# One kernel, one reordering: dense tile's first products ahead of two statistics, one root for both, the second half's routing four pairs later

## The reference, cut to what matters

```python
x = _layernorm(x + state_space(x))     # x_norm -> silu, sigmoid gates, a scan over time, W_out; it returns x + y
x = _layernorm(x + experts(x))         # 64 experts of 88 inner values, 8 chosen of each token, and a shared one
x = _layernorm(x + attention(x))       # 16 heads
x = _layernorm(x + signed_mlp(x))
# experts:
scores = sigmoid(x @ gate_w.T)                        # tokens x 64
# the four best of eight groups of experts, then the eight best experts in them
topk_w = scores[chosen]; topk_w = topk_w / (sum(topk_w) + 1e-20) * 2.5
routed = sum over the chosen e of topk_w[e] * (silu(x @ Wg[e].T) * (x @ Wu[e].T)) @ Wd[e].T
out = routed + shared_mlp(x)
```

## Time and profile before

| | us |
|---|---|
| median of 3 runs | 871.46 |
| the 3 runs | 866.16, 871.46, 871.61 |
| profiled execution, its own time | 871.87 |
| span of the profiled execution | 870.1 |
| busy in the span: PE / DVE / ACT / POOL | 621.8 / 483.9 / 400.0 / 365.4 |
| mean granted clock of TensorE | 0.844 of full speed |
| dense tile's pairs, first to last instruction of PE | from about 50 to 226 |
| the 56 and the 64 scatters of POOL | from 50 to 125 and from 156 to 237 |

### The profile page before, as it was taken

How to read it: one execution, slowest core, us unless ns; L and a number is a source line. 1 busy time by engine, 2 the same in 40 slices (tenths; PEclk the granted TensorE clock), 3 DMA queues, 4 the chain that set the end, 5 groups by cost and what they waited for, 6 DMA issues and landing times.

```text
span 870.1 us, 13130 instructions
## 1 busy us (share of the span) xinstructions
PE 621.8 (71%) x3712; PEld 388.1 (45%) x3713; DVE 483.9 (56%) x1238; ACT 400.0 (46%) x900; POOL 365.4 (42%) x401
## 2 busy tenths in 40 slices
PE   5671119510179999921978887967978999998995
PEld 2451006310058999921978772222322333343443
DVE  5770105300046666500646579775866888867986
ACT  4420103200034666600535557745755777787651
POOL 4157750677720000175040525787477070013552
PEclk9886558755579999965989977898989999999998
DMA  9999510211103666621555544242142131000001
GB/s 286 367 253 332 173 40 2 87 54 51 48 1 86 174 177 172 183 76 56 160 136 150 150 136 124 71 130 59 47 128 52 29 105 57 1 2 0 2 12 38
DMA packets 98716, 91.52 MB, mean 105 GB/s; under 512 B 9872, under 2 KB 83696, under 8 KB 97776
## 3 DMA queue, kind: packets, MB, share of 16 engines
q1 hardware_dynamic: 90704, 75.01, 29.4%
q0 software_dynamic: 7680, 15.74, 6.3%
q10 hardware_dynamic: 288, 0.23, 0.1%
HBM read 45.14 MB, written 45.61 MB: 104 GB/s over the span
## 4 chain that ended last, share of the span: by engine, by line
PE 51%; another core or an unknown queue 16%; DVE 13%; issue 11%; ACT 4%; POOL 2%; DMA 1%; SPq 0%; POOLq 0%; DVEq 0%; ACTq 0%
PE ps L1617 8%; PE ps L1604 6%; PE ps L1722 6%; PE ps L1732 6%; PE ps L1712 5%; DVE mx L1226 4%; PE ps L1612 3%; PE ps L1627 3%; PE ps L1526 2%; PE ps L1531 2%; ACT big L803 2%; DVE arena L1344 1%; DVE st L900 1%; DVE arena L1336 1%
## 5 line engine op out<-in xcount | busy, mean ns | idle before, releaser
L1226 DVE TENSOR_REDUCE mx<-ps 128x2 f32<-128x1024 f32 x128 | 151.0, 1217 | 51.0 <-PE ps L1712 31.0
L803 ACT ACTIVATE big<-ps 128x512 f32<-128x512 f32 x256 | 141.5, 598 | 68.7 <-PE ps L1722 45.3
L542 POOL DMA_INDIRECT xd<-xt,idx x120 | 116.1, 967 | 70.0 <-issue 35.8
L558 POOL DMA_INDIRECT big<-od,idx x72 | 69.4, 964 | 181.0 <-DMA od<-big 121.1
L1722 PE MATMUL ps<-arena 128*128 128x512 bf16 (+1 forms) x256 | 90.1, 402 | 24.1 <-ACT big L803 12.5
L1531 PE MATMUL ps<-arena,hmT 96*128 96x128 f32 x128 | 27.2, 346 | 112.1 <-issue 107.8
L1148 DVE TENSOR_TENSOR hm<-sg,ps 128x176 f32<-128x176 f32 x124 | 41.7, 336 | 114.3 <-ACT sg L741 82.4
L1617 PE MATMUL ps<-arena,xbT 128*128 x496 | 101.3, 329 | 5.4 <-issue 5.4
L1604 PE MATMUL ps<-arena,hmT 96*128 x496 | 81.1, 288 | 28.5 <-ACT hmT L737 25.7
L731 ACT ACTIVATE big<-ps 128x256 f32<-128x256 f32 x124 | 47.5, 383 | 83.6 <-PE ps L1604 49.8
L1604 PEld LDWEIGHTS ps<-arena,hmT 96*128 96x128 f32 x496 | 68.9, 200 | 32.6 <-issue 31.2
(11 more groups left out here) (222 smaller groups left out, 1087.7 us busy)
## 6 DMA issues: line engine op xcount, KB each, us to landing
big<-xd SPq DMA_DIRECT2D x62, 256.0 KB
od<-big SPq DMA_DIRECT2D x62, 256.0 KB
arena<-scr SPq DMA_DIRECT2D x96, 96.0 KB
xd<-zeros SPq DMA_DIRECT2D x1, 8192.0 KB
xd<-zeros SPq DMA_DIRECT2D x1, 7680.0 KB, 30.7
arena<-w_gu SPq DMA_DIRECT2D x4, 1408.0 KB, 21.1
arena<-w_d SPq DMA_DIRECT2D x4, 768.0 KB, 18.1
scr<-places SPq DMA_DIRECT2D x8, 384.0 KB
```

Of the source, the lines that this page charges most:

```text
L542: pool.indirect_dma_start(out=xd[f], out_offset=bass.IndirectOffsetOnAxis(ap=idx[:, t, k:k + 1], axis=0), in_=xt[:, t], in_offset=None).th ...
L558: pool.indirect_dma_start(out=slot[:, k], out_offset=None, in_=od[f], in_offset=bass.IndirectOffsetOnAxis(ap=idx[:, t, k:k + 1], axis=0)). ...
L803: act.activation(ering[:, HG * (mt % 2) + h], ps[:, 4 + h % 2, :], ACT.Exp, scale=SCALE).then_inc(exp_ready, 1)
L1226: v.tensor_reduce(mx[:, k, TB * h + 2 * a:TB * h + 2 * a + 2], ps[:, 2 * a:2 * a + 2, :], AX_X, ALU.max).then_inc(s1_free, 1)
```

## The change

The sums `2x + mixer` of quarters 2 and 3 are made first (`mix`, with a semaphore s_mix of their own), and their statistics are moved behind the dense pairs 0 and 1. PE's steps 1 and 2 wait for s_mix and no longer for the statistics. One `rstd_of_second_half` makes the roots of both quarters (8 columns instead of 4), after 6 scatters; before there were two, after 2 and 4 scatters. `normalise` of the two quarters moves from pairs 1 and 3 to pairs 5 and 7. All that belongs to the second half in `DENSE_BESIDE` and `ACT_BESIDE` moves four steps on, `ROUTED_FROM` goes from 8 to 12, and the `beside` steps of `route(1)` with it, so that s_eid of half 0 follows pair 11, and the first row numbers of the second half follow pair 28.

```diff
--- before.py
+++ after.py
@@ -86,9 +86,9 @@
     LOADS = {0: (2,), 1: (3,), 2: (4, 5), 3: (6,), 4: (7,), 6: (8, 9), 7: (10,), 8: (11,), 10: (12, 13), 11: (14,), 12: (15,)}
     MINE = MINGLED
-    DENSE_BESIDE = {4: 2, 6: 3, 8: "logits", 20: "places"}
-    ACT_BESIDE = {4: 2, 6: 3, 9: "scores"}
-    ROUTED_FROM = 8
+    DENSE_BESIDE = {8: 2, 10: 3, 12: "logits", 24: "places"}
+    ACT_BESIDE = {8: 2, 10: 3, 13: "scores"}
+    ROUTED_FROM = 12
     WEIGHT_PIECES = 4
     EP = E // WEIGHT_PIECES
     EARLY = NPAIR - 16
@@ -144,7 +144,7 @@
         st = sb("st", [P, NT, 6])
         mv = sb("mv", [P, NT, 2])
         rstd = sb("rstd", [P, NT])
-        minus_half = sb("minus_half", [P, TB])
+        minus_half = sb("minus_half", [P, 2 * TB])
         idf = sb("idf", [P, P])
         idb = sb("idb", [P, P], BF16)
         marks = sb("marks", [P, 2], BF16)
@@ -289,7 +289,7 @@
         th_ready, th_copied, d_ready, acc_done = sem("th_ready"), sem("th_copied"), sem("d_ready"), sem("acc_done")
         dg_ready, dsg_ready, dhm_ready = sem("dg_ready"), sem("dsg_ready"), sem("dhm_ready")
         dth_ready, dth_copied, dense_ready = sem("dth_ready"), sem("dth_copied"), sem("dense_ready")
-        s_pads, s_under = sem("s_pads"), sem("s_under")
+        s_pads, s_under, s_mix = sem("s_pads"), sem("s_under"), sem("s_mix")
         s_qk, s_qks, s_part, s_split = sem("s_qk"), sem("s_qks"), sem("s_part"), sem("s_split")
         s_pw = [sem(f"s_pw{o}") for o in range(2)]
         s_stk = [sem(f"s_stk{r}") for r in range(2 * GB)]
@@ -484,7 +484,14 @@
                 tiles = tiles_of(k)
                 r = rstd[:, tiles]
                 own(pool.tensor_scalar(r, mv[:, tiles, 1], EPS, None, ALU.add))
-                pool.tensor_tensor(r, r, minus_half[:], ALU.pow).then_inc(s_rstd, 1)
+                pool.tensor_tensor(r, r, minus_half[:, 0:TB], ALU.pow).then_inc(s_rstd, 1)
+
+            def rstd_of_second_half():
+
+                pool.wait_ge(s_st, 2 * B)
+                r = rstd[:, NT // 2:NT]
+                own(pool.tensor_scalar(r, mv[:, NT // 2:NT, 1], EPS, None, ALU.add))
+                pool.tensor_tensor(r, r, minus_half[:], ALU.pow).then_inc(s_rstd, 2)
             own(pool.memset(minus_half[:], -0.5))
             own(pool.memset(zeros[:], 0.0))
@@ -534,8 +541,8 @@
                         pool.wait_ge(s_idx, f + 1)
                     for k in range(TOP_K):
                         n = TOP_K * (t - FIRST[f]) + k
-                        if f == 0 and n in (2, 4):
-                            rstd_of(B + 1 + n // 2)
+                        if f == 0 and n == 6:
+                            rstd_of_second_half()
                         flying = AHEAD_ROWS[f]
                         if n >= flying:
                             pool.wait_ge(s_sc[f][n % flying], 16 * (n // flying))
@@ -943,11 +950,20 @@
                     ins = v.tensor_tensor(made[:, h], ps[:, bank, 0:2 * P].rearrange("p (j l) -> p j l", j=2), zT[:, c, h], ALU.mult)
                 ins.then_inc(s_ys, 1)
+            def mixed(q):
+
+                v.wait_ge(s_yo, q + 1)
+                return v.scalar_tensor_tensor(out=tmp[:, TB * q:TB * q + TB], in0=xt[:, TB * q:TB * q + TB], scalar=2.0,
+                                              in1=ps[:, q].rearrange("p (t m) -> p t m", m=M), op0=ALU.mult, op1=ALU.add)
+
             def add_mixer(q):
-                v.wait_ge(s_yo, q + 1)
-                own(v.scalar_tensor_tensor(out=tmp[:, TB * q:TB * q + TB], in0=xt[:, TB * q:TB * q + TB], scalar=2.0,
-                                           in1=ps[:, q].rearrange("p (t m) -> p t m", m=M), op0=ALU.mult, op1=ALU.add))
+
+                own(mixed(q))
                 stats(tmp, B + q)
+
+            def mix(q):
+
+                mixed(q).then_inc(s_mix, 1)
             first_stats(0)
             first_stats(1)
@@ -1063,7 +1079,7 @@
                 if f == 0:
                     gated(2)
                     gated(3)
-                beside(*range(ROUTED_FROM + 10, 22))
+                beside(*range(ROUTED_FROM + 10, ROUTED_FROM + 14))
                 if f == 0:
                     v.wait_ge(s_pos, 1)
                 else:
@@ -1071,34 +1087,39 @@
                 totals = ps[:, LOGITS[0], n * E:(n + 1) * E] if f == 0 else ps[:, 7, 0:E]
                 own(v.tensor_scalar(rows_of[:], totals, (P - 1) / 2.0, WHOLE_BLOCKS, ALU.add, ALU.add))
-                beside(22)
+                beside(ROUTED_FROM + 14)
                 own(v.tensor_tensor_scan(ends[:, 1:E + 1], back[:], rows_of[:], 0.0, ALU.add, ALU.add))
-                beside(23)
+                beside(ROUTED_FROM + 15)
                 v.wait_ge(s_pos, f + 1)
                 own(v.tensor_tensor(ch[:, own_ts], ps[:, LOGITS[f], 0:n * E].rearrange("p (t e) -> p t e", e=E),
                                     ends[:, 0:E].unsqueeze(1).broadcast_to([P, n, E]), ALU.add))
-                beside(24)
+                beside(ROUTED_FROM + 16)
                 own(v.max(dst[:, FIRST[f]], ch[:, FIRST[f]]))
                 v.tensor_scalar(idx[:, FIRST[f]], dst[:, FIRST[f]], -CHOSEN, None, ALU.add).then_inc(s_first, 1)
                 for t in tiles[1:]:
                     ins = v.max(dst[:, t], ch[:, t])
                 own(ins)
-                beside(25)
+                beside(ROUTED_FROM + 17)
                 rest_of = slice(FIRST[f] + 1, FIRST[f] + n)
                 v.tensor_scalar(idx[:, rest_of], dst[:, rest_of], -CHOSEN, None, ALU.add).then_inc(s_idx, 1)
-                beside(26, 27)
+                beside(ROUTED_FROM + 18, ROUTED_FROM + 19)
                 if f == 0:
-                    add_mixer(2)
-                    add_mixer(3)
+                    mix(2)
+                    mix(3)
                     own(v.scalar_tensor_tensor(out=ra[:, 0], in0=rb[:, 0], scalar=TAKEN, in1=sc[:, 0], op0=ALU.is_equal, op1=ALU.mult))
                     own(v.tensor_reduce(cnt[:, 0:1], ra[:, 0], AX_X, ALU.add))
                     own(v.tensor_scalar(cnt[:, 0:1], cnt[:, 0:1], 1e-20, None, ALU.add))
                     own(v.reciprocal(cnt[:, 0:1], cnt[:, 0:1]))
                     own(v.tensor_scalar(rw0[:], ra[:, 0], cnt[:, 0:1], ROUTED_SCALE, ALU.mult, ALU.mult))
                     for i in range(ROUTED_FROM):
-                        if i in (1, 3):
-                            normalise(xt, tmp, B + 2 + i // 2)
+                        if i == 1:
+                            v.wait_ge(s_mix, 2)
+                            stats(tmp, B + 2)
+                        if i == 2:
+                            stats(tmp, B + 3)
+                        if i in (5, 7):
+                            normalise(xt, tmp, B + 2 + i // 6)
                         dense(i)
                 for c in range(COLS[f]):
@@ -1107,7 +1128,7 @@
                     own(v.tensor_reduce(eidf[:, col], ecmp[:], AX_X, ALU.add))
                     own(v.tensor_scalar(eid[:, col], eidf[:, col], float(E - 1), None, ALU.min))
                 v.sem_inc(s_eid, 1)
-                beside(*range(28, E // 2))
+                beside(*range(ROUTED_FROM + 20, E // 2))
             route(0)
             route(1)
@@ -1520,7 +1541,7 @@
                         beside(DENSE_BESIDE[i])
                     if i < E // 2:
                         if 1 <= i < 3:
-                            pe.wait_ge(s_st, B + i + 2)
+                            pe.wait_ge(s_mix, i)
                         if i >= 3:
                             pe.wait_ge(dhm_ready, i - 2)
                         pe.matmul(ps[:, 1 + i % 3, 0:2 * I2], xT[:, 0:P], wgu_s[:, 2 * i:2 * i + 2, :].rearrange("p e n -> p (e n)"),
```

## The result

The changed kernel takes 866.11 us in the median of 21 runs, the kernel before 870.21 us in 21 runs on the same chips: a ratio of 0.9954, with an interval of 0.9934 to 0.9973. The change gains 4.1 us, where 0.3% more was forecast. The profiled execution of after took 861.22 us with a span of 859.5, against 871.87 and 870.1 before; of the 10.6 us between the spans 6.3 are there at the first product of the routed blocks. Most of the rest is the attention's: its score products last 234.3 us from first to last start instead of 240.2.

The account below looks back on a forecast made before the run. POOL's two fixed-length scatter streams, under which PE's increments arrive late, and the gap between them were taken as the bound. 871.87 + 5.8 - 2.9 = 874.8, predicted as 874.4 us for the median; range 864 to 883.

Parts of the forecast that it names:

- more slips through: Faster rival: all four pairs pass under the first scatter stream, gap 4.2 us shorter, late increments end sooner; 865 us, chance 0.18.
- a second stream before 157 us: Sign of being wrong: second half's scatters starting before 157 us, where 160 to 163 was forecast.
- The earlier start is worth nothing there ... One pair ahead.: First stream: the root holds pair 5 to 61.3 to 62.3 us; PE at step 9, not 8, when the crawl begins.
- +5.8: Delay in us of the second scatter stream: 4.2 pairs, 1.9 logits, 0.5 DVE routing, less 0.8 from POOL.
- Two of them: -2.9 us.: Refund behind the second stream: PE at shared tile 3 instead of 1, two tiles at 1.47 us each.
- Root: POOL's one break for the eight-column root costs 1.3 to 2.35 us; stream 1 ends 0.3 to 1.3 earlier, taken 0.8.
- SP's queue: s_eid of half 0 follows pair 11, at 109 to 131 us, delaying the second half's clear; costed 0, otherwise 1 to 2.
- Its rival: The clear holds the second stream: POOL starts at 165 us instead of 161, total 878 us, chance 0.07.
- the refills beside the gap: Instruction refills sharing transfer engines with a clear in the gap between streams could cost PE 0 to 4 us; taken 0.
- Crawl in the first six scatters: Slower rival: lateness near 57 us leaves PE at step 6; condition two 4 us increments before 60; 881.3 us, chance 0.20.
- Behind 270 us: Sign of being wrong: any stage after 270 us changing length, as the rest was expected to move as a whole.
- A wash: Rival: work under the streams counts by time, not increments, so PE's total is unchanged; 871.5 us, chance 0.13.

Follow-up runs that it names:

- the tables alone: Kernel before with only turns, logits, scores and routing moved four pairs later: 872.56 us against 874.58 (0.9992) with the long waits, ratio 1.0003 without.
- a late clear: Kernel before with the second half's buffer zeros issued only after scatter 48 of the first half has landed: 669.64 us, ratio 1.0209, without long waits.

## Why the prediction was wrong

The result, 866.11, lies in the range of 864 to 883, but on the other side of no change, and nearest to the rival "more slips through" (865, at 0.18). Of that rival only the gap came true, three pairs of four and for another reason: its brake, DVE waiting for the scores, was still there (51.97 us, until 125.92), and the last late wait still ended at 244.27 us, 7.3 us after the last scatter. That its number fits is luck. The picture of the kernel held: two ways of working, increments of PE that come late under POOL's streams, two streams of fixed length, and a gap whose end sets the rest. One of the signs of being wrong that the prediction names came up, a second stream before 157 us (156.32). Two steps of the sum failed.

**"The earlier start is worth nothing there ... One pair ahead."** The first half of the reasoning was measured as said: pair 5 at 61.84 us (forecast 61.3 to 62.3), `normalise` in front of it, waiting 2.61 us for the root. What I didn't work out was how fast PE goes on from there. With the turns at 62.67 and 65.77 and the logits behind pair 11, nothing stands between the pairs, and they follow each other each 1.26 to 1.84 us until 67.89: PE has begun pairs 0 to 11 where before it had begun 0 to 8, three ahead and not one. And I had left the onset at 65 to 67 us, where before had it, although I had moved the break: in after the break ends at 60.96, the first "remote" wait is that before 68.11 (1.04 us), and the first of over 2 us that before 70.97. The traces show that the quiet time moves with the break. With the tables alone the break ends at 58.08 us; there PE's turn of quarter 2, ended at 63.48, is copied 1.9 us later, and its next turn of a pair, ended at 65.26, 5.0 us later. In after the turn of quarter 3, ended at 66.37, is copied 1.7 us later, and the next turn of a pair, ended at 68.05, 2.9 us later. Counted from the end of the break, the first is sent after 5.4 us in both, the second after 7.2 and 7.1. Three pairs ahead instead of one leave 4 - 3 = 1 pair for the gap, 1.4 us, and no logits (they come at 72.84, under the stream); with the 0.5 of DVE and stream 1 ending 0.4 us earlier (124.10 against 124.52) the term would have been +1.5 and not +5.8. It measured +0.2: the last late copy under the stream came 1.3 us earlier than before (123.53 against 124.78), which nothing in the change aims at.

The tables alone are the test of this step: without the early products and the later break pair 10 begins only at 73.04, the turn of quarter 3 is copied at 80.95 among late ones, and the second stream started 4.7 us later. Hence the halves don't add up: the tables put four more pairs ahead of the routing, and only the earlier products and the later break get them through before the onset. How the two share it was not tested; two profiles, one of each kernel, put them about even. Counted from the first scatter, the break ends at 9.9 us in after and at 8.1 with the tables alone, and pair 9 begins at 13.3 us and at 15.1. Whether one root or two makes a difference there stays open: the change with two roots ran only without the long waits, where it made none.

**"Two of them: -2.9 us."** The refund was 6.0 us for the tables alone and, for the whole change, 6.7 (26.4 us from the end of the stream at 237.0 to 263.4, against 33.1). I had counted nine late increments at three a shared tile and let the rest of the dense tile eat some. But dense pair 31 is begun at 157.65, before the second onset; shared tile 4 is begun at 174.19, and from there a tile comes each 13.4 to 22.4 us (tiles 5 to 8 at 187.62, 207.92, 230.32 and 247.84), a long wait and one of 5 us in turn. Before, most of that stretch went to the dense tail, with one wait of 13 to 16.4 us for each copy, at 190.83, 207.63 and 224.43 us. At the end PE stands at tile 8 where it stood at tile 3 (247.84 against 248.19), five tiles ahead and not two: the term is mis-sized, -6.7 in the place of -2.9. As I read these rows, late increments don't have one price, and those of the dense tail were the dear ones.

With the first step alone put right the sum would have been 1.5 - 2.9 = -1.4, with the second alone 5.8 - 6.7 = -0.9; with both, -5.2, where the profiles have -6.3 and the medians -4.1.

The smaller steps. *Root*: a break that costs 1.3 to 2.35 us was forecast; from the end of one scatter to the next it was 2.33 (58.63 to 60.96), so 2.0 more than the usual 0.30, nearer to the upper end than I took it. The root itself took 1.68 us, between the 1.05 of a pure overhead and the 2.1 of a time that scales. Stream 1 ended 0.4 us earlier, though it had begun 0.7 later (51.05 against 50.38). *SP's queue*: s_eid was expected at 105 to 131 us and came ahead of 74.61, because pair 11 was through. Its rival and the refills beside the gap (the Trainium skill, "DMA: Bandwidth & Descriptors", Queues, rings and completion order) had nothing left to act on, the DMA share in the gap being 0.01; what a late clear costs, 15.4 us, its own experiment shows. *Crawl in the first six scatters*: 7.6 us without a break made one increment late, by a microsecond (the product of pair 5 ended at 58.40, its silu began at 59.64), and the break came; its condition was not met. *Behind 270 us*: a stage there did change its length in the profile, the attention, by 5.9 us; it is the spread between single executions told above. *A wash*: that PE's total is unchanged is true, and doesn't decide, since time under the streams counts by increments.

What I call late increments was argued in the prediction and is now better founded. In before POOL's gathers, from 366 us on, are a third stream; it has PE's turn of 378.96 us (0.63 long), and its copy by DVE starts at 400.19 (DVE was held by another instruction until 395.28, and then waited 4.91 us more); ACT's copy at 386.89 lets PE start at 387.42, 0.15 us after its end:

```profile
378.96 0.63 PE L1627 MATMUL ps<-idf,big 128*128 128x128 f32 x2
387.42 1.22 PE L1604 MATMUL ps<-arena,hmT 96*128 x4 [7.83 <-ACT hmT L737]
```

```profile
386.89 0.38 ACT L737 ACTIVATE hmT<-ps 96x256 f32<-96x256 f32 x1 [3.05 <-remote]
```

```profile
400.19 0.42 DVE L1152 COPY xbT<-ps 128x256 f32<-128x256 f32 x1 [4.91 <-remote]
```

What PE sends is late, what is sent to PE is not. The Trainium skill, "Perfetto Trace Analysis", Per-instruction lifecycle, says that the propagation of a semaphore lies outside the window that the profiler reports; that fits waits of which the profile knows no releaser. Whether the increment leaves PE late or travels long isn't visible, nor why whole series of runs have it and others don't.

## What to carry to other kernels

Where a stretch of a kernel crawls, count what gets through ahead of its onset, event by event with the real pitch, and don't stop at the first event that is unchanged; two edits that are each worth nothing can be worth something together when one makes the work and the other makes the room. Find out first whether the kernel has another way of running, for an edit has to be weighed in both: with the breaks the changed kernel ran 63 us below the kernel before in one and 16 above it in the other. Where it can be arranged, have POOL issue many indirect transfers in a row only while no other engine waits for TensorE.

## What the runs showed of the hardware

- The same program takes 870 or 654 us. The 216 us between them go with waits for what TensorE sends while GpSimd issues indirect transfers back to back, many of them of 5.3 or of 13 to 16.5 us, the longest 28.34 us; the granted clock is down at 0.51 to 0.58 there. One chip had a series of each kind. What decides between them stays open. (A single run of before among 13 took 857.72 us, where the other twelve took 651 to 657; its clock, 0.65, is not that of the 870 us kind, 0.84 to 0.86, and no trace of it was kept.)
- With breaks of GpSimd of 1.7 us after every eight scatters the changed kernel ran 63 us below the kernel before with the long waits and 16 us above it without, in one run each, so it is no version that is better in both. With plain transfers of GpSimd it ran 142 us below, in one run; with two transfers under way instead of eight it took 864.56 us against 865.29, in one run each.
- With the long waits, the first increment that is late by more than a microsecond was sent 5 to 10 us after an unbroken stream began.
- Neither the clear nor busy transfer engines are needed for it: with the tables alone the waits begin at 70 us at a DMA share of 0.16, the clear going out at 107.
- GpSimd's power of -1/2 takes 1.05 us over 128x4 and 1.68 us over 128x8. A clear of 7680 KB took 29.0 to 32.5 us to land in the twenty profiles, issued between 67 and 116 us.
